# Reordering one GpSimd addition and one ScalarE copy, and reducing softmax's maximum and sum in one operation each

## The chip, the cores and the metric

One core of one Trainium2 chip runs the whole program. The metric is device time in microseconds, the median of several runs. The engines are TensorE (PE in the profile, its weight loads PEld), VectorE (DVE), ScalarE (ACT), GpSimd (POOL) and the DMA queues (SP issues most of them). Each engine runs its own instructions in the order in which they are written; they meet only at semaphores.

## What is computed

The input is `x` of 4 sequences of 2048 rows of 256 float32 values. The result is a sandwich of three residual layers:

```
x = x + 0.5 * ffn(layernorm(x))     # gate: top 2 of 8 experts, each 256x256
x = x + attn(layernorm(x))          # 16 heads of 16; a row attends to itself and its two neighbours
x = x + 0.5 * ffn(layernorm(x))     # the same weights as the first

idx    = stack([(i - 1) % s, i, (i + 1) % s], axis=1)
scores = einsum('bshd,bsnhd->bshn', q, k[:, idx])      # three scores for each row and head
attn   = softmax(scores, axis=-1)
out    = einsum('bshn,bsnhd->bshd', attn, v[:, idx])
```

The experts are all computed and then weighted by a gate that is zero for the six not chosen. Softmax is over three values, so the kernel holds `score` and `prob` as [128 rows, 3, 2 x 16]: the three neighbours stand 32 values apart.

## The kernel before

The 8192 rows are 64 tiles of 128, handled as 32 pairs. A software pipeline of 37 steps (`s` from -1 to 35) runs over the pairs; the program is unrolled. In one step the engines work on several pairs at once: the first FFN of pair s, the attention projections of pair s-1, scores of group s-2, the output projection and the third layer norm of group s-3, and the second FFN of group s-4. A step in the middle of the kernel is a fixed, hand-written order of calls for each engine.

TensorE, in a middle step (`body`, last block): first FFN t=0 (24 matmuls of 512 columns), transposes TA, first FFN t=1, the 16 gate matmuls (L930), transposes TO, q/k/v (24 matmuls), output projection (12 matmuls into tr_bank), gate transpose (L939), second FFN's first bank, bias matmuls (L955), 24 more matmuls, transposes TD, 18 more, transposes TB. All FFN products go through four PSUM banks, `ffn_bank`, so the next product into a bank waits until ScalarE (even banks, `scale_step`, L446) or VectorE (odd banks, `chain_step`, L656) has read it. Every product is made of a high and a low part: ScalarE copies the transposed operand rounded to `T_hi` (`hi_step`, L409), VectorE subtracts it to get `T_lo` (`lo_step`, L579), and TensorE waits for `T_lo`. The output projection waits for `T_lo` of TO (L579), which VectorE makes in the middle of the gate's chain of small operations (L593 to L636).

VectorE, in a middle step: the second half of softmax (`weights_step(s-3, 1)`, L707 to L713), first FFN's sums (`chain_step`, which for its first bank needs GpSimd's `base`), values (L724 to L736), the gate, norm statistics, scores (L678 to L688), second FFN's sums, and between them the first half of softmax (`weights_step(s-2, 0)`: maximum L699, L701; subtraction L703), then `T_lo` of TD.

GpSimd, in a middle step: sums of the first FFN, then `rstd` of the second and third norms with `base` of the second FFN between them, `x1_bo`, `rstd` of the first norm for pair s+2 (ends with L314), then the sums of the second FFN (`sum_step`, L332, L334, L340, twice), then `base_step(FFN1, s+1)` (L324), then two gathers of rows of x (L383).

ScalarE, in a middle step: ..., `scale_step(FFN2, s-4, 0)`, `normalise_step(LN3, s-3)`, `exp_step(s-2)` (L487, waits for the subtraction L703), `hi_step(TD, s-3)` (waits for TensorE's transposes TD), `scale_step(FFN2, s-4, 1)` (L446), `hi_step(TB, s)`.

At the end (steps 31 to 33) VectorE runs both halves of softmax and the value step within one step (`drains`), since there is no further pair to hide them behind. From step 32 on there is no first FFN.

`idle` (L558) is a two-element copy that keeps two dependent VectorE operations apart.

Of the kernel before, what the change touches and what calls it, by code (L numbers as in the profile page):

```python
# [22 lines left out]
B, S, D, H, E = 4, 2048, 256, 16, 8  # L23
DH = D // H
PART = 128
# [52 lines left out]
def build(nc, x, Wp, bp, Wq, bq, Wk, bk, Wv, bv, Wo, bo, We, be, Wg, bg, out):  # L78
# [9 lines left out]
    with ExitStack() as ctx:  # L88
        def sb(name, shape, dt=f32):
            return ctx.enter_context(nc.sbuf_tensor(name, shape, dt))  # L90
# [63 lines left out]
        moved_x1_bo = sb("moved_x1_bo", [PART, 2, D])  # L154
        prod = sb("prod", [PART, 3, 2, D])
        score, prob = sb("score", [PART, 3, 2 * H]), sb("prob", [PART, 3, 2 * H])
        most = sb("most", [PART, 2, 2 * H])
        total = sb("total", [PART, 3, 2 * H])
        attn = sb("attn", [PART, 2, D])
        x2 = sb("x2", [PART, 2, 2, D])  # L160
        y = sb("y", [PART, 2, 2, D])
# [115 lines left out]
        def _(pool):  # L277
# [38 lines left out]
            def base_step(f, n):  # L316

                if f == FFN1:
                    await_x(pool, n)
                else:  # L320
                    pool.wait_ge(x2_done, n.times(1, 1))
                pool.wait_ge(bias_copied[f], n.times(1, 1))
                await_(pool, chain_done[f], n.times(8))
                nc.gpsimd.tensor_tensor(base[:, f], (x_in if f == FFN1 else x2)[:, n.slot], bias_sum[:, f],  # L324
                                        ALU.add).then_inc(base_done[f], 1)
# [32 lines left out]
            def body(s):  # L358
# [9 lines left out]
                    x1_bo_step(s - 1)  # L368
                if (s + 2).within(PAIRS):
                    rstd_step(LN1, s + 2)  # L370
                if (s - 4).within(GROUPS):
                    sum_step(FFN2, s - 4, 0)
                    sum_step(FFN2, s - 4, 1)
                if (s + 1).within(PAIRS):
                    base_step(FFN1, s + 1)
                n = s + 3
                if n.within(PAIRS):
                    if n.const == 2:
# [12 lines left out]
        def _(act):  # L391
# [114 lines left out]
            def body(s):  # L506
# [31 lines left out]
                    scale_step(FFN2, s - 4, 0)  # L538
                if (s - 3).within(GROUPS):
                    normalise_step(LN3, s - 3)  # L540
                if (s - 2).within(GROUPS):
                    exp_step(s - 2)
                if (s - 3).within(GROUPS):
                    hi_step(TD, s - 3)
                if ffn2:
                    scale_step(FFN2, s - 4, 1)
                if ffn1 and not filling:
# [6 lines left out]
        def _(dve):  # L554
# [136 lines left out]
            def weights_step(a, part):  # L691
                ops = attn_ops

                def after(k):
                    dve.wait_ge(ops, a.times(ATTN_OPS, k))

                if part == 0:
                    after(4)
                    nc.vector.tensor_tensor(most[:, 0], score[:, 0], score[:, 1], ALU.max).then_inc(ops, 1)  # L699
                    after(5)  # L700
                    nc.vector.tensor_tensor(most[:, 1], most[:, 0], score[:, 2], ALU.max).then_inc(ops, 1)  # L701
                    after(6)
                    nc.vector.tensor_tensor(score[:], score[:], most[:, 1].unsqueeze(1).to_broadcast([PART, 3, 2 * H]),  # L703
                                            ALU.subtract).then_inc(ops, 1)
                else:
                    dve.wait_ge(exp_done, a.times(1, 1))
                    nc.vector.tensor_tensor(total[:, 0], prob[:, 0], prob[:, 1], ALU.add).then_inc(ops, 1)  # L707
                    after(8)
                    nc.vector.tensor_tensor(total[:, 1], total[:, 0], prob[:, 2], ALU.add).then_inc(ops, 1)
                    after(9)  # L710
                    nc.vector.reciprocal(total[:, 2], total[:, 1]).then_inc(ops, 1)
                    after(10)
                    nc.vector.tensor_tensor(prob[:], prob[:], total[:, 2].unsqueeze(1).to_broadcast([PART, 3, 2 * H]),  # L713
                                            ALU.mult).then_inc(ops, 1)

            def value_step(a):
# [365 lines left out]
```

## Time and profile before

| | us |
|---|---|
| median of 3 runs | 1137.74 (1134.66 to 1139.28) |
| the profiled execution, its own time | 1135.11 |
| its span from first to last instruction | 1133.3, mean granted TensorE clock 0.976 |
| busy: TensorE matmul | 1070.8 (94%) |
| busy: TensorE weight load | 889.8 (79%) |
| busy: VectorE | 950.8 (84%) |
| busy: GpSimd | 714.8 (63%) |
| busy: ScalarE | 518.8 (46%) |

A matmul of 512 columns is listed as 0.39 us long, but the next one starts 0.23 us later: the listed times overlap, and a busy TensorE is not a TensorE without gaps. Gaps are read from the starts of its instructions, one after the other. A row of the timeline gives start, duration, engine, line, operation, what is written and read, the count, and in brackets the idle time before it and what ended that. A row of the chain gives start, duration and what. In the page's second part the granted clock of TensorE is full through the middle and falls at the start and in the last tenth of the span.

### The profile page before, as it was taken

The numbers are of one execution on the slowest core, as the hardware profiler recorded it, in microseconds if no ns is written. First come the engines' busy times: TensorE is split into PE (matmuls) and PEld (weight loads), VectorE is DVE, ScalarE is ACT, GpSimd is POOL, SyncE is SP. The second block draws the span as 40 slices with busy tenths as digits, with TensorE's granted clock in tenths as the row PEclk, the third lists the DMA queues.
The fourth block names the chain that finished last, engine by engine and source line by source line (L and its number), as shares of the span: only waits on it lengthen the run. The fifth ranks groups of instructions, "written<-read, shape, count | busy, mean of one in ns | idle before, by whom it ended". The sixth has DMA issues, their size and how long they took to land.

```text
span 1133.3 us, 17965 instructions
## 1 busy us (share of the span) xinstructions
PE 1070.8 (94%) x5459; PEld 889.8 (79%) x5459; DVE 950.8 (84%) x2675; ACT 518.8 (46%) x1181; POOL 714.8 (63%) x953
## 2 busy tenths in 40 slices
PE   4898799999999999999999999999999999998785
PEld 2676688888888888888888888888888888887563
DVE  3659789898898898888888989888889898988873
ACT  3253454444455544544555444445554444444331
POOL 2465466666676666666766676667666766563443
PEclk9899899999999999999999999999999999999988
DMA  5001000000000000000000000000000000000000
GB/s 162 10 30 35 12 15 6 19 20 20 19 19 20 14 6 19 20 19 20 20 19 11 10 19 20 19 20 19 20 12 8 19 20 20 10 10 10 10 10 19
DMA packets 12583, 23.05 MB, mean 20 GB/s; under 512 B 2212, under 2 KB 5812, under 8 KB 12488
## 3 DMA queue, kind: packets, MB, share of 16 engines
q1 hardware_dynamic: 9240, 13.37, 3.4%
q0 software_dynamic: 3248, 8.54, 2.7%
q8 instruction: 44, 0.72, 0.3%
q14 instruction: 51, 0.42, 0.1%
HBM read 12.47 MB, written 8.39 MB: 18 GB/s over the span
## 4 chain that ended last, share of the span: by engine, by line
PE 80%; DVE 9%; SPq 3%; DMA 2%; issue 2%; ACT 2%; POOL 1%; DVEq 0%; POOLq 0%; ACTq 0%
PE ffn_bank L889 18%; PE ffn_bank L891 18%; PE ffn_bank L890 18%; PE tr_bank L918 5%; PE tr_bank L930 4%; PE mix_bank L890 3%; PE mix_bank L891 3%; PE mix_bank L889 3%; SPq L243 2%; PE tr_bank L889 2%; DVE chain_sum L656 2%; PE mix_bank L955 1%; DMA we_raw<-in_L_ffn_We 1%; PE tr_bank L891 1%; PE tr_bank L890 1%
## 5 line engine op out<-in xcount | busy, mean ns | idle before, releaser
L889 PE MATMUL ffn_bank<-we_hi,T_hi 128*128 128x512 f32 x1024 | 416.3, 407 | 3.8 <-DVE chain_sum L656 2.5
L891 PE MATMUL ffn_bank<-we_hi,T_lo 128*128 128x512 f32 x1024 | 404.9, 395 | 0.0
L890 PE MATMUL ffn_bank<-we_lo,T_hi 128*128 128x512 f32 x1024 | 404.0, 395 | 0.0
L332 POOL TENSOR_TENSOR chain_sum<-chain_sum,we_raw 128x512 f32<-128x512 f32 x128 | 165.8, 1295 | 184.4 <-DVE chain_sum L656 184.4
L446 ACT ACTIVATE we_raw<-ffn_bank,gate 128x256 f32<-128x256 f32 x512 | 208.1, 479 | 134.7 <-PE ffn_bank L891 134.6
L889 PEld LDWEIGHTS ffn_bank<-we_hi,T_hi 128*128 128x128 f32 x1024 | 195.3, 191 | 46.1 <-issue 4.6
L891 PEld LDWEIGHTS ffn_bank<-we_hi,T_lo 128*128 128x128 f32 x1024 | 194.5, 190 | 43.2
L890 PEld LDWEIGHTS ffn_bank<-we_lo,T_hi 128*128 128x128 f32 x1024 | 195.6, 191 | 35.5
L409 ACT CAST T_hi<-tr_bank 128x512 fp32r<-128x512 f32 x128 | 75.0, 588 | 121.8 <-PE tr_bank L918 121.6
L656 DVE SCALAR_TENSOR_TENSOR chain_sum<-ffn_bank,gate,base 128x256 f32<-128x256 f32 x128 | 61.4, 479 | 77.2 <-POOL base L324 49.3
L656 DVE SCALAR_TENSOR_TENSOR chain_sum<-ffn_bank,gate,chain_sum 128x256 f32<-128x256 f32 x256 | 110.7, 473 | 8.4 <-PE ffn_bank L891 8.4
L334 POOL TENSOR_TENSOR pool_sum<-chain_sum,we_raw 128x256 f32<-128x256 f32 x128 | 108.4, 847 | 10.0
L309 POOL TENSOR_TENSOR var_eps<-mean_var,eps 128x2 f32<-128x2 f32 x96 | 20.7, 216 | 144.1 <-DVE mean_var L574 144.1
L579 DVE TENSOR_TENSOR T_lo<-tr_bank,T_hi 128x512 fp32r<-128x512 f32 x128 | 87.0, 682 | 27.6 <-ACT T_hi L409 27.6
L889 PE MATMUL mix_bank<-wqkv_hi,T_hi 128*128 128x512 f32 (+1 forms) x256 | 90.1, 352 | 5.0 <-ACT qk L470 5.0
L558 DVE COPY idle<-minus_half 128x2 f32<-128x2 f32 x170 | 85.6, 504 | 5.9
L891 PE MATMUL mix_bank<-wqkv_hi,T_lo 128*128 128x512 f32 (+1 forms) x256 | 87.9, 343 | 0.0
L890 PE MATMUL mix_bank<-wqkv_lo,T_hi 128*128 128x512 f32 (+1 forms) x256 | 87.8, 343 | 0.0
L383 POOL DMA_INDIRECT x_in<-in_L_attn_x,x_row x60 | 66.9, 1115 | 18.2 <-issue 9.1
L312 POOL TENSOR_TENSOR rstd<-var_eps,minus_half 128x2 f32<-128x2 f32 x96 | 77.0, 802 | 0.0
L429 ACT ACTIVATE normed<-x,shift,rstd 128x256 f32<-128x256 f32 x128 | 70.6, 609 | 6.4 <-POOL shift L314 6.3
L918 PE MATMUL tr_bank<-ident,normed 128*128 128x128 f32 x384 | 59.9, 281 | 8.0 <-ACT normed L429 7.9
(128 smaller groups left out, 1862.2 us busy)
## 6 DMA issues: line engine op xcount, KB each, us to landing
out_x<-y SPq DMA_DIRECT2D x31, 256.0 KB, 2.0
we_raw<-in_L_ffn_We SPq DMA_DIRECT2D x2, 1024.0 KB, 13.9
x_in<-in_L_attn_x,x_row POOLq DMA_INDIRECT x60, 2.9
x_in<-in_L_attn_x SPq DMA_DIRECT2D x2, 256.0 KB, 7.5
moved_qk<-qk SPq DMA_DIRECT2D x4, 124.0 KB
w_raw<-in_L_attn_Wq SPq DMA_DIRECT2D x1, 256.0 KB, 2.8
w_raw<-in_L_attn_Wk SPq DMA_DIRECT2D x1, 256.0 KB, 3.0
w_raw<-in_L_attn_Wv SPq DMA_DIRECT2D x1, 256.0 KB, 3.9
```

The costliest lines, as they stand in the source:

```text
L312: nc.gpsimd.tensor_tensor(rstd[:, ln], var_eps[:, ln], minus_half[:], ALU.pow).then_inc(done, 1)
L332: nc.gpsimd.tensor_tensor(chain_sum[:, f, t], chain_sum[:, f, t], scaled[:, f, t, 1], ALU.add).then_inc(done, 1)
L334: nc.gpsimd.tensor_tensor(pool_sum[:, f, t], chain_sum[:, f, t, 0], scaled[:, f, t, 0, 1], ALU.add).then_inc(done, 1)
L409: nc.scalar.copy(halves(i, n)[0][:].rearrange("p t k n -> p (t k n)"), t_bank[i][:, :]).then_inc(hi_done[i], 1)
L446: last = nc.scalar.activation(scaled[:, f, t, half, j], ffn_bank[b][:, j * D:(j + 1) * D], ACT.Copy, scale=gate[:, 2 * f + t, e:e + 1])
L558: nc.vector.tensor_copy(idle[:], minus_half[:])
L579: nc.vector.tensor_tensor(lo[:].rearrange("p t k n -> p (t k n)"), t_bank[i][:, :], hi[:].rearrange("p t k n -> p (t k n)").bitcast(f32), ...
L656: nc.vector.scalar_tensor_tensor(out=chain_sum[:, f, t, j], in0=ffn_bank[b][:, j * D:(j + 1) * D], scalar=gate[:, 2 * f + t, e:e + 1], in1 ...
L889: nc.tensor.matmul(dest, hi[:, t, k, :], w_hi_[:, k, c0:c1], start=(first and k == 0), stop=False, skip_group_check=not first)
L890: nc.tensor.matmul(dest, hi[:, t, k, :], w_lo_[:, k, c0:c1], start=False, stop=False, skip_group_check=not first)
L891: last = nc.tensor.matmul(dest, lo[:, t, k, :], w_hi_[:, k, c0:c1], start=False, stop=(k == KB - 1), skip_group_check=not first)
L918: last = nc.tensor.transpose(t_bank[i][:, at:at + PART], source[:, t, k * PART:(k + 1) * PART], ident[:])
```

## The change

Four edits. GpSimd's `base_step(FFN1, s + 1)` moves in front of the two `sum_step(FFN2, ...)`. ScalarE's `hi_step(TD, s - 3)` moves in front of `exp_step(s - 2)`. The maximum over the three scores becomes one `tensor_reduce` along a view in which the three are innermost (stride 32 values), in place of two `tensor_tensor`; so does the sum over the three exponentials. The semaphore's counts stay as they were (the reduction adds 2).

```diff
@@ gpsimd, body
                     rstd_step(LN1, s + 2)
+                if (s + 1).within(PAIRS):
+                    base_step(FFN1, s + 1)
                 if (s - 4).within(GROUPS):
                     sum_step(FFN2, s - 4, 0)
                     sum_step(FFN2, s - 4, 1)
-                if (s + 1).within(PAIRS):
-                    base_step(FFN1, s + 1)
@@ scalar, body
                     normalise_step(LN3, s - 3)
+                if (s - 3).within(GROUPS):
+                    hi_step(TD, s - 3)
                 if (s - 2).within(GROUPS):
                     exp_step(s - 2)
-                if (s - 3).within(GROUPS):
-                    hi_step(TD, s - 3)
@@ vector, weights_step
                     after(4)
-                    nc.vector.tensor_tensor(most[:, 0], score[:, 0], score[:, 1], ALU.max).then_inc(ops, 1)
-                    after(5)
-                    nc.vector.tensor_tensor(most[:, 1], most[:, 0], score[:, 2], ALU.max).then_inc(ops, 1)
+                    nc.vector.tensor_reduce(most[:], score[:].rearrange("p m h -> p h m"), AX.X, ALU.max).then_inc(ops, 2)
                     after(6)
...
                     dve.wait_ge(exp_done, a.times(1, 1))
-                    nc.vector.tensor_tensor(total[:, 0], prob[:, 0], prob[:, 1], ALU.add).then_inc(ops, 1)
-                    after(8)
-                    nc.vector.tensor_tensor(total[:, 1], total[:, 0], prob[:, 2], ALU.add).then_inc(ops, 1)
+                    nc.vector.tensor_reduce(total[:, 0], prob[:].rearrange("p m h -> p h m"), AX.X, ALU.add).then_inc(ops, 2)
                     after(9)
```

The subtraction, the reciprocal and the multiplication that follow read `most` and `total` at their new places and are otherwise the same.

## Rows read from the trace of the kernel before

**Rows 1.** Windows: busy us and (count) of PE, PEld, DVE, ACT, POOL; clock; DMA
```profile
483.00:516.00 33.00, 33.00 (x174) 27.71 (x172) 29.29 (x82) 15.76 (x36) 23.09 (x30) 1.00 0.05 17
```

**Rows 2.** Timeline of PE, step 13: gate matmuls, projection, second FFN's first bank
```profile
432.00 0.28 PE L930 MATMUL tr_bank<-wg,T_hi 128*128 128x16 f32 x2
...
438.48 0.39 PE L889 MATMUL tr_bank<-wo_hi,T_hi 128*128 128x256 f32 x1
...
440.18 0.47 PE L889 MATMUL ffn_bank<-we_hi,T_hi 128*128 128x512 f32 x1
```

**Rows 3.** Timeline of PE, step 4: the same three instructions
```profile
140.94 0.28 PE L930 MATMUL tr_bank<-wg,T_hi 128*128 128x16 f32 x2
...
147.34 0.28 PE L889 MATMUL tr_bank<-wo_hi,T_hi 128*128 128x256 f32 x1
...
148.81 0.48 PE L889 MATMUL ffn_bank<-we_hi,T_hi 128*128 128x512 f32 x1
```

**Rows 4.** Timeline of DVE: first gate operation in step 4, then step 13 with T_lo
```profile
142.82 0.19 DVE L593 TENSOR_TENSOR logits<-tr_bank,bg_all 128x32 f32<-128x32 f32 x1 [0.81 <-PE tr_bank L930]
...
434.64 0.17 DVE L593 TENSOR_TENSOR logits<-tr_bank,bg_all 128x32 f32<-128x32 f32 x1
...
437.75 0.68 DVE L579 TENSOR_TENSOR T_lo<-tr_bank,T_hi 128x512 fp32r<-128x512 f32 x1
```

**Rows 5.** Waits, whole span: who waited for whom, us in total, times, longest
```profile
DVE chain_sum L656 <- POOL base L324: 49.3, 28, 2.0
```

**Rows 6.** Timeline of POOL, step 13: last rstd operation, base addition
```profile
448.46 0.19 POOL L314 TENSOR_TENSOR shift<-minus_mean,rstd 128x2 f32<-128x2 f32 x1
...
458.18 1.29 POOL L324 TENSOR_TENSOR base<-x_in,bias_sum 128x512 f32<-128x512 f32 x1
```

**Rows 7.** Timeline of PE: transposes TD, TB, TB and the matmul behind them
```profile
447.67 0.66 PE L918 MATMUL tr_bank<-ident,normed 128*128 128x128 f32 x4
448.08 0.49 PE L889 MATMUL ffn_bank<-we_hi,T_hi 128*128 128x512 f32 x1
...
452.31 0.60 PE L918 MATMUL tr_bank<-ident,normed 128*128 128x128 f32 x4
453.46 0.47 PE L889 MATMUL ffn_bank<-we_hi,T_hi 128*128 128x512 f32 x1 [0.55 <-ACT we_raw L446]
...
485.30 0.60 PE L918 MATMUL tr_bank<-ident,normed 128*128 128x128 f32 x4
485.79 0.47 PE L889 MATMUL ffn_bank<-we_hi,T_hi 128*128 128x512 f32 x1
```

**Rows 8.** Timelines of POOL, DVE and ACT, step 13: sum, maximum, subtraction, exponential, T_hi, scaling
```profile
449.57 1.29 POOL L332 TENSOR_TENSOR chain_sum<-chain_sum,we_raw 128x512 f32<-128x512 f32 x1 [0.92 <-DVE chain_sum L656]
...
449.62 1.29 DVE L701 TENSOR_TENSOR most<-most,score 128x32 f32<-128x32 f32 x1
450.94 0.84 DVE L703 TENSOR_TENSOR score<-score,most 128x96 f32<-128x96 f32 x1
...
451.82 0.29 ACT L487 ACTIVATE prob<-score 128x96 f32<-128x96 f32 x1 [4.21 <-DVE score L703]
452.01 0.57 ACT L409 CAST T_hi<-tr_bank 128x512 fp32r<-128x512 f32 x1
452.47 0.48 ACT L446 ACTIVATE we_raw<-ffn_bank,gate 128x256 f32<-128x256 f32 x1
```

**Rows 9.** The chain that ended last, steps 31 and 32
```profile
1031.17 1.30 DVE most L701
...
1033.44 0.85 ACT we_raw L446 x2
...
1042.06 0.43 PE mix_bank L890
```

**Rows 10.** Source lines L688 and L707: count, ns min/median/max, first and last start, form
```profile
L688 DVE TENSOR_REDUCE score<-prod x32: 1733/1740/1753, 95.6 to 1079.2; 128x96 f32<-128x1536 f32 x32
...
L707 DVE TENSOR_TENSOR total<-prob x32: 178/908/921, 98.8 to 1086.5; 128x32 f32<-128x32 f32 x32
```

More of the change, by code:

```diff
@@ L156, in build @@
         score, prob = sb("score", [PART, 3, 2 * H]), sb("prob", [PART, 3, 2 * H])
-        most = sb("most", [PART, 2, 2 * H])
-        total = sb("total", [PART, 3, 2 * H])
+        most = sb("most", [PART, 2 * H])
+        total = sb("total", [PART, 2, 2 * H])
         attn = sb("attn", [PART, 2, D])
@@ L698, in weights_step @@
                     after(4)
-                    nc.vector.tensor_tensor(most[:, 0], score[:, 0], score[:, 1], ALU.max).then_inc(ops, 1)
-                    after(5)
-                    nc.vector.tensor_tensor(most[:, 1], most[:, 0], score[:, 2], ALU.max).then_inc(ops, 1)
+                    nc.vector.tensor_reduce(most[:], score[:].rearrange("p m h -> p h m"), AX.X, ALU.max).then_inc(ops, 2)
                     after(6)
-                    nc.vector.tensor_tensor(score[:], score[:], most[:, 1].unsqueeze(1).to_broadcast([PART, 3, 2 * H]),
+                    nc.vector.tensor_tensor(score[:], score[:], most[:].unsqueeze(1).to_broadcast([PART, 3, 2 * H]),
                                             ALU.subtract).then_inc(ops, 1)
@@ L706, in weights_step @@
                     dve.wait_ge(exp_done, a.times(1, 1))
-                    nc.vector.tensor_tensor(total[:, 0], prob[:, 0], prob[:, 1], ALU.add).then_inc(ops, 1)
-                    after(8)
-                    nc.vector.tensor_tensor(total[:, 1], total[:, 0], prob[:, 2], ALU.add).then_inc(ops, 1)
+                    nc.vector.tensor_reduce(total[:, 0], prob[:].rearrange("p m h -> p h m"), AX.X, ALU.add).then_inc(ops, 2)
                     after(9)
-                    nc.vector.reciprocal(total[:, 2], total[:, 1]).then_inc(ops, 1)
+                    nc.vector.reciprocal(total[:, 1], total[:, 0]).then_inc(ops, 1)
                     after(10)
-                    nc.vector.tensor_tensor(prob[:], prob[:], total[:, 2].unsqueeze(1).to_broadcast([PART, 3, 2 * H]),
+                    nc.vector.tensor_tensor(prob[:], prob[:], total[:, 1].unsqueeze(1).to_broadcast([PART, 3, 2 * H]),
                                             ALU.mult).then_inc(ops, 1)
```

## The prediction

> **What bounds the kernel now.** I read the windows first, in stretches of 33 us, one step of the pipeline each. In the middle of the kernel TensorE is busy for 33.00 of 33.00 us at full clock, VectorE for 29.3, GpSimd for 23.1, ScalarE for 15.8 [rows 1]; the 26 windows from 153 to 1011 us are all like this one, with never less than 32.45 us of TensorE. Taken at its word this says that no other engine matters there, and that the change can only help at the two ends. But matmuls overlap in the record, so a gap of some tenths between two of them does not show as idle time. So I read TensorE's timeline by the starts of its instructions, and compared the same piece of work in different steps.
>
> Two places in the middle are longer than the work in them. The first lies around the output projection. From the first gate matmul to the second FFN's first matmul takes 440.18 - 432.00 = 8.18 us in step 13 [rows 2] and 148.81 - 140.94 = 7.87 us in step 4 [rows 3], for the same 16 gate matmuls, transposes, q/k/v, projection and gate transpose at the same clock. The difference, 0.31 us, has a cause in the row of VectorE: the projection starts at 438.48 [rows 2], and `T_lo`, its operand, was finished at 437.75 + 0.68 = 438.43 [rows 4]. TensorE waits for VectorE there. VectorE is late because it comes late to the gate: its first gate operation starts 434.64 - 432.00 = 2.64 us behind the first gate matmul in step 13, against 142.82 - 140.94 = 1.88 us in step 4, where it sat waiting for TensorE [rows 2 to 4].
>
> The second place is the end of a step. Behind the transposes TD the next matmul starts after 448.08 - 447.67 = 0.41 us; behind the transposes TB after 0.49 us in step 14, and after 1.15 us in step 13, where the row itself names ScalarE's L446 as what it waited for [rows 7]. Of the 23 such transitions I read (steps 6 to 28), these are the shortest and the longest; their mean is 0.58 us, 0.17 us over the 0.41.
>
> What stands before that L446 is a chain [rows 8]: second maximum (L701, from 449.62), subtraction (L703), exponential, `T_hi` of TD, then L446 at 452.47. It takes 2.85 us. In the drain, the same chain takes 1033.44 - 1031.17 = 2.27 us, and there it is on the chain that ended last [rows 9].
>
> **The base addition.** VectorE waits for it in 28 steps, 49.3 us in total, up to 2.0 us [rows 5]. The addition runs at 458.18, though the last `rstd` operation in front of its new place ends at 448.46 + 0.19 = 448.65 [rows 6] and its inputs (x gathered in an earlier step, the bias copied before the second norm's scaling) are there. At its new place it runs at about 448.7 to 450.0. What is queued behind it: the first of the FFN2 sums, which now starts at 449.57 [rows 8], moves by 0.4 us; the outputs' stores hang on it, and nothing on TensorE. The gathers stand behind the sums as before and no longer have the addition right ahead of them, so they are not later. VectorE's wait goes. What is late next for it: TensorE's own banks. Its first gate operation then comes as soon as the logits do, 1.88 instead of 2.64 us behind [rows 3, 4], and `T_lo` is up to 0.76 us earlier, where the projection lacks only some 0.3. So the projection's stall goes: 0.31 us in steps 5 to 31, 27 x 0.31 = 8.4 us.
>
> **The maximum.** L701 takes 1.29 us for 32 elements, and ends with GpSimd's L332 (449.57 + 1.29 = 450.86; L701 ends at 450.91). The subtraction then takes 0.84 us in the face of the next GpSimd sum [rows 8]. So it is not arithmetic that is paid here but the wait of an operation with two inputs for GpSimd. The new reduction has one input. The nearest row is L688, 1.74 us for 1536 elements to 96 sums, with hardly any scatter (1733 to 1753 ns) although it meets GpSimd's work too [rows 10]. That bounds the reduction of 96 elements to 32 results: 1.74 x 96 / 1536 = 0.11 us if elements count, 1.74 x 32 / 96 = 0.58 us if results count. I take 0.25, nearer to the lower end since a result here has 3 elements and not 16. Either way it ends while GpSimd's sum runs, and the subtraction (two inputs) inherits the 1.29 us wait. What is saved is the second operation of the pair: from the start of L701 to L446 there remain 1.29 + 0.04 to the exponential and, with `T_hi` out of the way, 0.19 to L446, together 1.52 us. That is 2.85 - 1.52 = 1.33 us less where the subtraction met GpSimd a second time, 2.27 - 1.52 = 0.75 us less where it didn't [rows 8, 9].
>
> The Trainium skill says the same of the wait ("Advanced Engine Details and Errata", GPSIMD Details): GpSimd shares a read and a write interface with VectorE, in conflict with VectorE instructions that have two SBUF inputs. By that rule the wait passes on to the subtraction; without it the drain's gain below would be some 3.7 us larger.
>
> **ScalarE's copy ahead of the exponential.** It waits for the transposes TD, which start at 447.67 and are over before 448.4 [rows 7], when the exponential can't start before about 450. ScalarE is idle for 4.21 us there [rows 8]. So the copy costs nothing at its new place; the 0.46 us between its start and L446 (452.47 - 452.01) are in the 1.33 and 0.75 above. If the transposes were later than the score, the exponential would wait behind the copy; by these rows they have 1.5 us in hand.
>
> Together these two edits bring L446 0.75 to 1.33 us forward, over the 0.74 us (1.15 - 0.41) that TensorE waited at the worst. So the stall behind TB goes: 27 steps (4 to 30) x 0.17 = 4.6 us.
>
> **The sum of the exponentials.** In the middle VectorE meets GpSimd there (median 0.91 us), in the drain it doesn't (0.18) [rows 10]. Two additions of 0.18 give way to one reduction of 0.11 to 0.58: between 0.25 us gained and 0.22 lost for each of three drain steps; at 0.25 for the reduction it is 0.1 each, 0.3 in all. In the middle the slack above hides it.
>
> The Trainium skill speaks against these views ("Vector Engine (DVE) Microarchitecture Reference", 5.2 Measured stream behaviour on trn2): a stream in single words with steps between them falls to 2.5 ns per column. An estimate by that page is 0.32 us for a reduction, and 0.1 us instead of 0.3 us gained in the drain. No row here shows such a stream.
>
> **The ends.** In the filling steps the base addition does not move past anything (there is no second FFN yet) and what ends last is the transfer of the moved q and k, which does not depend on softmax; I count nothing. In steps 31 to 33 the softmax chain is on the path: 0.75 us in each of 31 and 32 [rows 9], and 1.33 in 33, which repeats the form of rows 8. That is 2.8 us, with the sum 3.1.
>
> **The sum.** 1135.1 (the profiled execution) - 8.4 - 4.6 - 3.1 = 1119.0 us. The median of the runs shown is 2.6 us above that execution; I forecast 1119, 1.6% below the median.
>
> **The rivals.**
> One stall stays (1124 to 1128): the base addition now runs into the moment when the subtraction wants its turn, and if GpSimd's next sum gets in first, as at 450.94 [rows 8], the subtraction waits a second time, and the stall behind TB stays: 1135.1 - 8.4 - 3.1 = 1123.6. Or VectorE, early now, has its value products fall on GpSimd's sums and gives the time back before the gate: 1135.1 - 4.6 - 3.1 = 1127.4. Against it: L701 waited and got its turn as soon as L332 ended.
>
> Drain alone (1132): the middle is bound by TensorE as the windows say [rows 1], and my 0.31 and 0.17 us are its own way of starting, not waits: 1135.1 - 3.1 = 1132.0. Against it speaks that `T_lo` ends 0.05 us before the projection starts [rows 2, 4].
>
> Slower (about 1155): the reduction over three strided elements is dear. The chain from the first maximum to L446 takes about 2.5 us in the shorter form (2.27 from the second maximum [rows 9], and some 0.2 for the first); with a reduction of R it takes R + 0.5. From R = 2.0 us the stall behind TB grows by what lies above, in 27 steps; with the projection's gain set against it, the kernel is slower from R = 2.3. At R = 3 it is 27 - 8.4 = 19 us slower. The bound of 0.58 from L688 speaks against it.
>
> Clock: behind idle gaps of some us in the drain a matmul comes every 0.43 us instead of 0.23, nine in a row at 1042 [rows 9], 1.8 us for each such stretch. Shorter gaps may spare one or two, moved ones may add one: 1115 to 1121.
>
> **Chances.** Forecast 0.50, forecast with stretches at half clock spared 0.06 (1115), one stall stays 0.24, drain alone 0.14, slower 0.06. The range has to leave out no more than 0.2: 1113 to 1132, where the upper end takes in the drain alone in part. A measurement of this kernel can tell about 0.5% from no change; against the median that is 1132.05, so the drain alone falls half and half: faster 0.50 + 0.06 + 0.24 + 0.07 = 0.87, same 0.07, slower 0.06.
>
> **What would show it.** In the profile after, VectorE's wait for L324 is gone from the waits; the projection starts 0.12 us after the last v matmul and `T_lo` is over some tenths before; behind TB the next matmul starts after 0.41 us; a middle step lasts some 0.5 us less. L703 takes about 1.3 us and ends with a GpSimd operation; the reductions take 0.2 to 0.4 us. It is wrong if the middle steps keep their length, or if a reduction takes over a microsecond.

## The result and the profile after

The changed kernel takes 1116.49 us (median of 6 runs, 1115.0 to 1119.13) beside 1136.62 us for the kernel before (6 runs, 1133.9 to 1139.49). The ratio is 0.982, with a 95% interval of 0.980 to 0.985: 1.8% faster. The forecast was 1119.0 us. The profiled execution took 1119.13 us with a span of 1117.1 us, beside 1135.11 and 1133.3 before. It is the slowest of the six, and the one before is faster than the median: the medians are 20.1 us apart, the two profiles 16.0. What follows divides up the 16.0; about the other 4 us no trace says anything.

First the page of the changed kernel, busy us of each engine and its share of the span:

```profile
PE 1055.4 (94%) x5459; PEld 884.0 (79%) x5459; DVE 904.2 (81%) x2611; ACT 528.1 (47%) x1181; POOL 714.0 (64%) x953
```

Then the window that [rows 1] shows of before (columns as there):

```profile
483.00:516.00 33.00, 33.00 (x175) 27.95 (x175) 28.20 (x83) 17.29 (x39) 23.37 (x31) 1.00 0.05 17
```

TensorE is busy for 33.00 of 33.00 us in both kernels, and yet a step of the pipeline has become shorter. The windows can't show this, since they don't see tenths between overlapping matmuls. The starts do. TensorE's timeline after, step 13 of the pipeline (start, us, line, operands), against [rows 2, 7]:

```profile
429.43 0.28 PE L926 MATMUL tr_bank<-wg,T_hi 128*128 128x16 f32 x2
...
435.82 0.28 PE L885 MATMUL tr_bank<-wo_hi,T_hi 128*128 128x256 f32 x1
...
437.29 0.48 PE L885 MATMUL ffn_bank<-we_hi,T_hi 128*128 128x512 f32 x1
...
449.42 0.60 PE L914 MATMUL tr_bank<-ident,normed 128*128 128x128 f32 x4
449.77 0.48 PE L885 MATMUL ffn_bank<-we_hi,T_hi 128*128 128x512 f32 x1
```

From the first gate matmul to the second FFN's first matmul it now takes 437.29 - 429.43 = 7.86 us; before it took 8.18 there and 7.87 in step 4 [rows 2, 3]. Behind the transposes TB the next matmul starts after 449.77 - 449.42 = 0.35 us, not 0.49 to 1.15 [rows 7]. The other engines in the same step:

```profile
429.63 0.88 DVE L656 SCALAR_TENSOR_TENSOR chain_sum<-ffn_bank,gate,chain_sum 128x256 f32<-128x256 f32 x2 [1.19 <-PE ffn_bank L887]
431.31 0.19 DVE L593 TENSOR_TENSOR logits<-tr_bank,bg_all 128x32 f32<-128x32 f32 x1 [0.81 <-PE tr_bank L926]
433.51 0.68 DVE L579 TENSOR_TENSOR T_lo<-tr_bank,T_hi 128x512 fp32r<-128x512 f32 x1
...
445.72 1.30 POOL L324 TENSOR_TENSOR base<-x_in,bias_sum 128x512 f32<-128x512 f32 x1
446.98 1.31 POOL L332 TENSOR_TENSOR chain_sum<-chain_sum,we_raw 128x512 f32<-128x512 f32 x1
...
446.53 0.24 DVE L699 TENSOR_REDUCE most<-score 128x32 f32<-128x96 f32 x1
446.81 0.32 DVE L701 TENSOR_TENSOR score<-score,most 128x96 f32<-128x96 f32 x1
...
445.48 0.59 ACT L409 CAST T_hi<-tr_bank 128x512 fp32r<-128x512 f32 x1 [0.75 <-PE tr_bank L914]
447.17 0.28 ACT L487 ACTIVATE prob<-score 128x96 f32<-128x96 f32 x1 [1.10 <-DVE score L701]
447.36 0.46 ACT L446 ACTIVATE we_raw<-ffn_bank,gate 128x256 f32<-128x256 f32 x1
```

VectorE's first gate operation starts 431.31 - 429.43 = 1.88 us behind the first gate matmul, and it sat waiting for TensorE, as in step 4 before [rows 4]. `T_lo` ends at 434.19, 1.63 us ahead of the projection; before it was 0.05 [rows 2, 4]. The base addition stands at 445.72, directly ahead of the first FFN2 sum. `T_hi` is out of the way 1.1 us before the exponential, and L446 follows the exponential after 0.19 us instead of 0.65 [rows 8].

Over all middle steps (6 to 29), before and after: a step lasts 32.39 and 31.84 us. From gate to FFN2 it is 8.21 and 7.87, behind TB 0.58 and 0.35. The two places give 0.34 + 0.23 = 0.57, the step 0.55. The whole execution, by the gate transpose's copy (L421) of each step: up to step 4 149.1 and 151.1 us (+2.0), steps 4 to 30 842.0 and 827.7 (-14.2), step 30 to 31 31.4 and 30.5 (-0.9), from there to the end of the last arithmetic instruction 102.5 and 99.5 (-3.0). Behind it the last store and the end of the program take 8.4 us in both. Step 13, from which most rows of before are taken, is an unusual one: it is the only one of the middle steps 6 to 29 in which the subtraction L703 takes 0.84 us; in the others it takes 0.26.

### The profile page after: what moved, and what is told of

It reads as the page before. It is cut to its first block, busy times and chain, and to the rows that moved or that the text cites. A ratio compares the mean times of both kernels' runs of the same rounds, so it can differ in the third digit from the quotient of the medians.

```text
span 1117.1 us, 17965 instructions
## 1 busy us (share of the span) xinstructions
PE 1055.4 (94%) x5459; PEld 884.0 (79%) x5459; DVE 904.2 (81%) x2611; ACT 528.1 (47%) x1181; POOL 714.0 (64%) x953
## 4 chain that ended last, share of the span: by engine, by line
PE 84%; DVE 6%; SPq 3%; DMA 2%; issue 2%; ACT 1%; POOL 0%; POOLq 0%; DVEq 0%; ACTq 0%
PE ffn_bank L885 19%; PE ffn_bank L887 19%; PE ffn_bank L886 19%; PE tr_bank L914 5%; PE tr_bank L926 4%; PE mix_bank L885 4%; PE mix_bank L886 4%; PE mix_bank L887 4%; SPq L243 2%; PE tr_bank L885 1%; PE tr_bank L886 1%; PE tr_bank L887 1%; PE mix_bank L951 1%; DMA we_raw<-in_L_ffn_We 1%; DMA moved_x_bo<-x_bo 1%
## 5 line engine op out<-in xcount | busy, mean ns | idle before, releaser
L446 ACT ACTIVATE we_raw<-ffn_bank,gate 128x256 f32<-128x256 f32 x512 | 209.1, 473 | 139.3 <-PE ffn_bank L887 138.3
L309 POOL TENSOR_TENSOR var_eps<-mean_var,eps 128x2 f32<-128x2 f32 x96 | 20.6, 215 | 146.4 <-DVE mean_var L574 146.4
L334 POOL TENSOR_TENSOR pool_sum<-chain_sum,we_raw 128x256 f32<-128x256 f32 x128 | 104.4, 816 | 10.0
L324 POOL TENSOR_TENSOR base<-x,bias_sum 128x512 f32<-128x512 f32 x32 | 42.1, 1316 | 70.3 <-issue 55.7
L383 POOL DMA_INDIRECT x_in<-in_L_attn_x,x_row x60 | 71.6, 1193 | 15.2 <-issue 13.2
L558 DVE COPY idle<-minus_half 128x2 f32<-128x2 f32 x170 | 75.9, 447 | 5.9
```

Source lines behind the costliest of these rows:

```text
L334: nc.gpsimd.tensor_tensor(pool_sum[:, f, t], chain_sum[:, f, t, 0], scaled[:, f, t, 0, 1], ALU.add).then_inc(done, 1)
L383: nc.gpsimd.indirect_dma_start(out=x_in[:, n.slot, t, :], out_offset=None, in_=x_rows[:, :], in_offset=bass.IndirectOffsetOnAxis(ap=x_row[ ...
L446: last = nc.scalar.activation(scaled[:, f, t, half, j], ffn_bank[b][:, j * D:(j + 1) * D], ACT.Copy, scale=gate[:, 2 * f + t, e:e + 1])
L558: nc.vector.tensor_copy(idle[:], minus_half[:])
```

## The experiments

The forecast rests on two stalls of TensorE that are counted one by one: one that the late base addition causes (the projection, 8.4 us), one that softmax and ScalarE's copy cause (behind TB, 4.6 us). The kernels below make the parts alone or leave one out. All of them have the same arithmetic unless told otherwise. Medians in us; "before" is the kernel before, run alongside; steps are means over 6 to 29, "gate-FFN2" and "behind TB" the two places above. The drain (the copy of step 31 to the end of the last arithmetic) and the steps are of one profile each; the drain moves with the stretches in which the granted clock is half. Medians, not profiles, say which kernel is faster.

| kernel | median | before | ratio (95%) | step | gate-FFN2 | behind TB | drain |
|---|---|---|---|---|---|---|---|
| before | 1136.62 | | | 32.39 | 8.21 | 0.58 | 102.5 |
| base_only | 1139.4 | 1139.68 | 1.0008 (0.9989-1.0027) | 32.41 | 7.87 | 0.95 | 102.9 |
| hi_alone | 1121.41 | 1135.4 | 0.9867 (0.9851-0.9884) | 31.92 | 7.94 | 0.36 | 100.0 |
| max_alone | 1127.61 | 1135.4 | 0.9921 (0.9903-0.9939) | 32.17 | 8.17 | 0.38 | 101.6 |
| sum_alone | 1132.52 | 1135.4 | 0.9973 (0.9963-0.9982) | 32.48 | 8.17 | 0.72 | 100.6 |
| max_and_sum (one run) | 1124.56 | 1135.4 | | 32.11 | 8.11 | 0.38 | 99.5 |
| all_but_softmax | 1128.04 | 1139.68 | 0.9917 (0.9893-0.9941) | 32.16 | 7.87 | 0.70 | 99.8 |
| all_but_hi | 1117.95 | 1139.68 | 0.9824 (0.9799-0.9848) | 31.87 | 7.87 | 0.38 | 98.4 |
| all_but_base | 1117.54 | 1139.68 | 0.9826 (0.9801-0.9851) | 31.84 | 7.88 | 0.35 | 97.4 |
| after | 1116.49 | 1136.62 | 0.9824 (0.9802-0.9846) | 31.84 | 7.87 | 0.35 | 99.5 |

### The base addition alone (base_only)

```diff
 rstd_step(LN1, s + 2)
+base_step(FFN1, s + 1)
 sum_step(FFN2, s - 4, 0)
 sum_step(FFN2, s - 4, 1)
-base_step(FFN1, s + 1)
```

> The kernel before with the base addition moved and nothing else. Theory (two separate stalls of TensorE in a middle step: the projection's, set by VectorE that waited for the base addition, and the one behind the transposes TB, set by the softmax chain on ScalarE): the first goes, the second stays. A middle step of 32.39 us becomes 32.05 to 32.1, the drain keeps its length, about 1128 us where before has 1136.6. Rival (the base addition's 2 us were all of VectorE's lateness, everything follows from it): a middle step of 31.84 as in the changed kernel, about 1121 us.

Measured: 1139.4 beside 1139.68 us, ratio 1.0008. The projection's stall is gone in all steps (7.87 us), as the forecast had it, and the kernel is no faster. Neither the theory (32.05 to 32.1 us a step) nor the rival (31.84) came out: it is 32.41. The timelines of POOL, DVE, ACT and PE of this kernel, step 13 (its gate transpose's copy starts at 442.19):

```profile
450.34 1.29 POOL L324 TENSOR_TENSOR base<-x_in,bias_sum 128x512 f32<-128x512 f32 x1
451.59 1.29 POOL L332 TENSOR_TENSOR chain_sum<-chain_sum,we_raw 128x512 f32<-128x512 f32 x1
...
451.15 0.53 DVE L699 TENSOR_TENSOR most<-score 128x32 f32<-128x32 f32 x1
451.71 1.22 DVE L701 TENSOR_TENSOR most<-most,score 128x32 f32<-128x32 f32 x1
452.96 0.26 DVE L703 TENSOR_TENSOR score<-score,most 128x96 f32<-128x96 f32 x1
...
453.25 0.29 ACT L487 ACTIVATE prob<-score 128x96 f32<-128x96 f32 x1 [3.90 <-DVE score L703]
...
454.00 0.60 PE L918 MATMUL tr_bank<-ident,normed 128*128 128x128 f32 x4
454.90 0.47 PE L889 MATMUL ffn_bank<-we_hi,T_hi 128*128 128x512 f32 x1 [0.30 <-ACT we_raw L446]
```

The first maximum ends with the base addition (451.68 and 451.63), the second with the sum behind it (452.93 and 452.88). The pair needs 1.78 us and starts into one GpSimd operation more than before. The second half of L446 comes 11.7 to 11.9 us behind the copy of the gate transpose instead of 11.4 (medians of odd and even steps), and TensorE waits for it behind TB: 0.95 us on average instead of 0.58. What the projection gives, 0.34 us, TB takes, 0.37.

### All but the base addition (all_but_base)

The edit is the changed kernel with `base_step(FFN1, s + 1)` back behind the two FFN2 sums.

> The changed kernel with the base addition at its old place. Theory: the stall behind TB goes, the projection's stays, and the drain gains its 3 us: a middle step of about 32.15 us, about 1127 us. Rival (it is VectorE's work that counts, and the reductions take some 1.7 us per step of it away): VectorE reaches the gate early in spite of the wait, 31.84 us per step, about 1118 us.

Measured: 1117.54 beside 1139.68 us, ratio 0.9826, a middle step of 31.84 us, the same as with all four parts. The rival came out. The wait of VectorE for the base addition is not only still there, it is longer than in [rows 5]:

```profile
DVE chain_sum L656 <- POOL base L324: 78.5, 28, 2.9
```

(waits over the whole span: us in total, times, longest). It costs nothing now. VectorE comes 2.13 us behind the first gate matmul instead of 2.68, and `T_lo` is ready 0.49 us ahead of the projection on average instead of 0.06. The same kernel's timelines of DVE, ACT and POOL in step 13:

```profile
444.92 0.25 DVE L699 TENSOR_REDUCE most<-score 128x32 f32<-128x96 f32 x1
445.20 1.28 DVE L701 TENSOR_TENSOR score<-score,most 128x96 f32<-128x96 f32 x1
...
446.52 0.28 ACT L487 ACTIVATE prob<-score 128x96 f32<-128x96 f32 x1 [2.06 <-DVE score L701]
446.71 1.55 ACT L446 ACTIVATE we_raw<-ffn_bank,gate 128x256 f32<-128x256 f32 x4
...
445.08 1.29 POOL L332 TENSOR_TENSOR chain_sum<-chain_sum,we_raw 128x512 f32<-128x512 f32 x1 [0.92 <-DVE chain_sum L656]
...
452.35 1.30 POOL L324 TENSOR_TENSOR base<-x_in,bias_sum 128x512 f32<-128x512 f32 x1
```

Here the subtraction pays the 1.28 us as forecast (it ends at 446.48, GpSimd's sum at 446.37), and the base addition is still 7.3 us behind it. But it comes 16.4 us behind the gate transpose's copy and not 17.1: whatever brings L446 forward brings VectorE's sums, GpSimd's sums and with them the base addition forward.

### The copy alone (hi_alone)

```diff
 normalise_step(LN3, s - 3)
-exp_step(s - 2)
 hi_step(TD, s - 3)
+exp_step(s - 2)
```

> The kernel before with ScalarE's third-norm operand ahead of the exponential and nothing else. Theory now (one root: L446 of the second FFN's second half, held up by the softmax chain, delays both TensorE behind TB and, by way of VectorE's sums, GpSimd's sums and the base addition behind them, VectorE's start into the next step and so the projection): L446 comes 0.46 us earlier, the stall behind TB goes in the short form of the chain, the base addition comes up to 0.46 us earlier and most of the projection's stall goes too; a middle step of 31.9 to 32.0 us against 32.39 before and 31.84 after, the drain 1 to 1.4 us shorter, about 1122 us. Rival (two separate causes, the projection's stall needs the base addition moved): 32.15 to 32.2 us, about 1129 us.

Measured: 1121.41 beside 1135.4 us, ratio 0.9867, as this theory had it. A middle step takes 31.92 us: 0.47 of the 0.55 us come from exchanging two instructions of ScalarE. ScalarE's timeline, step 13, and TensorE's behind TB:

```profile
446.44 0.58 ACT L409 CAST T_hi<-tr_bank 128x512 fp32r<-128x512 f32 x1 [0.75 <-PE tr_bank L918]
449.30 0.28 ACT L487 ACTIVATE prob<-score 128x96 f32<-128x96 f32 x1 [2.28 <-DVE score L703]
449.49 1.55 ACT L446 ACTIVATE we_raw<-ffn_bank,gate 128x256 f32<-128x256 f32 x4
...
450.37 0.60 PE L918 MATMUL tr_bank<-ident,normed 128*128 128x128 f32 x4
450.72 0.48 PE L889 MATMUL ffn_bank<-we_hi,T_hi 128*128 128x512 f32 x1
```

L446 follows 0.19 us behind the exponential, with the copy long done. The first time of the second half moves from 11.4 to 10.9 us behind the gate transpose's copy. The same half microsecond can be followed round: the base addition goes from 17.1 to 16.6 us behind that copy and VectorE's first FFN1 sum of the next step from 18.5 to 18.0. TensorE, no longer held behind TB, is itself 0.2 us earlier at its next gate matmul (23.7 instead of 23.9 us behind the copy), so that of VectorE's 0.5 us there remain 0.3: its first gate operation goes from 2.68 to 2.39 us behind the gate matmul, and `T_lo` from 0.06 to 0.25 us ahead of the projection. So the place from gate to FFN2 shrinks to 7.94 us, by 0.27 of the 0.34, without the base addition being touched.

### The maximum, the sum, and both (max_alone, sum_alone, max_and_sum)

```diff
-nc.vector.tensor_tensor(most[:, 0], score[:, 0], score[:, 1], ALU.max).then_inc(ops, 1)
-after(5)
-nc.vector.tensor_tensor(most[:, 1], most[:, 0], score[:, 2], ALU.max).then_inc(ops, 1)
+nc.vector.tensor_reduce(most[:, 1], score[:].rearrange("p m h -> p h m"), AX.X, ALU.max).then_inc(ops, 2)
```

> The kernel before with the maximum as one reduction and nothing else. Theory of one root: the reduction takes 0.25 us, the subtraction takes over the wait for GpSimd (1.28 us), L446 comes 0.3 us earlier in the short form and 0.9 us in the long one, both stalls go nearly whole: 31.85 to 31.95 us per step, drain 1 to 1.5 us shorter, about 1121 us. Rival (two causes): 32.15 to 32.2 us, about 1129 us.

```diff
-nc.vector.tensor_tensor(total[:, 0], prob[:, 0], prob[:, 1], ALU.add).then_inc(ops, 1)
-after(8)
-nc.vector.tensor_tensor(total[:, 1], total[:, 0], prob[:, 2], ALU.add).then_inc(ops, 1)
+nc.vector.tensor_reduce(total[:, 1], prob[:].rearrange("p m h -> p h m"), AX.X, ALU.add).then_inc(ops, 2)
```

> The kernel before with the sum of the exponentials as one reduction and nothing else. Theory of one root: the 0.85 us per step that VectorE saves lie before its wait for the base addition, which grows by as much; the middle step stays at 32.39 us, the drain loses 0.1 us per step at most: within 1 us of before. Rival (VectorE's work counts): 32.1 to 32.2 us per step, about 1130 us.

The third kernel has both.

> The kernel before with both reductions and nothing else. Theory of one root: as with the maximum alone, 31.85 to 31.95 us per step, the sum adds nothing in the middle. Rival (the sum's 0.85 us count once the maximum is out of the way): at least 0.1 us per step less than with the maximum alone.

Measured: the maximum alone gives 0.22 us a step (32.17), nearly all of it behind TB (0.38 us). The subtraction takes 1.28 us in place of the second maximum and ends 0.22 us earlier, which is the first maximum saved; the base addition moves by 0.23 us and the place from gate to FFN2 by 0.04. This is what the rival with two causes had forecast (32.15 to 32.2 us), not the theory of one root. The reason stands in the starts: VectorE's first FFN1 sum is 0.23 us earlier, TensorE's next gate matmul 0.18, so only 0.05 us reach the gate (2.63 instead of 2.68). An earlier L446 shortens the projection's stall only by what it gives over TensorE's own gain behind TB.

The sum alone: in its profile a middle step is no shorter (32.48 us, +0.09), since the subtraction loses its turn to GpSimd more often (0.84 us in place of 0.26 in 6 of the 24 steps; in the kernel before in one), and behind TB it is 0.72 us. But that profile is of the slowest of its ten executions (1135.89 us), and the median is 2.9 us under before, with a ratio whose interval lies below 1. So the sum alone gains some 0.3%; no trace shows where. Both together: 32.11 us, 0.28 us a step.

### Leaving out the copy, and leaving out both reductions (all_but_hi, all_but_softmax)

Each is the changed kernel with one part as it was before: `exp_step` ahead of `hi_step(TD, ...)`, or the pairs of maxima and additions.

> The changed kernel with ScalarE's third-norm operand behind the exponential again. Theory: L446 comes some 0.46 us later than in the changed kernel, which the middle has in hand, so 31.84 to 31.9 us per step; the drain loses 3 x 0.46 = 1.4 us: about 1118 us against 1116.5. Rival (the copy's place is what removed the stall behind TB): 32.05 us per step, about 1124 us.

> The changed kernel with the two-operation maximum and sum. Theory: 31.84 to 31.95 us per step, since the copy's new place alone is worth 0.46 us against a mean stall of 0.2; the drain keeps 3 x 0.46 of its 3 us: about 1118.5 us. Rival (the second maximum's wait for GpSimd, now with the base addition in front of the sums, keeps ScalarE late): 32.05 us per step, about 1124 us.

Measured: 1117.95 and 1128.04 us beside 1139.68, ratios 0.9824 and 0.9917; 31.87 and 32.16 us a step. The first is as its theory had it; the second is slower than theory and rival. Without the copy's move the kernel loses 0.03 us a step, though that move alone gave 0.47. Without the reductions, base addition and copy together give 0.23 us, less than the copy alone (0.47): with the pair of maxima the early base addition costs 0.24 us a step. With the reductions it is the other way round: they give 32.11 us without it (max_and_sum) and 31.87 with it (all_but_hi). There the exponential starts 9.6 to 9.7 us behind the gate transpose's copy instead of 10.5, because the subtraction gets in between the base addition and the sum and doesn't wait a whole GpSimd operation. That brings L446 early enough without the copy's move, so copy and early addition stand in for each other. So the parts don't add. Alone they give -0.02, 0.47, 0.22 and -0.09 us, a sum of 0.58 that is close to the 0.55 of all four only by chance: copy, maximum and sum without the base addition already give 0.55. By the ratios of whole executions the four alone give 1.3, 0.8, 0.3 and -0.1%, together 2.3, and all four at once 1.8%.

### What the base addition is good for (slack_all, slack_no_base)

Both get a needless reduction of `prod` (1.74 us on VectorE, its result is not used) in each middle step, behind the values' sum and ahead of the first FFN's sums of the second tile.

```diff
+filler = sb("filler", [PART, 96])
...
+if s.const < PAIRS - 1:
+    nc.vector.tensor_reduce(filler[:], prod[:].rearrange("p m t (h d) -> p (m t h) d", d=DH), AX.X, ALU.add)
```

On the changed kernel:

> The changed kernel with one more reduction of 1.74 us on VectorE in every middle step, behind the values' sum (its result is not used). Theory: in the changed kernel VectorE waits 1.1 us for TensorE at its next sum but one and has the projection's operand ready 1.6 us ahead; together more than 1.74, so a middle step stays at 31.84 us. Rival (VectorE is close to its limit): the step grows by 0.2 us or more.

On all_but_base:

> The same extra reduction of 1.74 us in the kernel that has everything but the moved base addition. Theory: the step was 31.84 us there too, but the operand was ready only 0.44 us ahead and VectorE did not wait for TensorE; so the step grows by 1.74 - 0.44 = 1.3 us, to about 33.1 us, and the moved addition is worth its margin alone. Rival (the moved addition is of no use at all): as in the run beside it.

Measured, one run each: 1118.65 and 1155.03 us, a middle step of 31.84 and 33.28 us. The changed kernel takes up 1.74 us a step and shows nothing of it; without the base addition's move 1.43 us of it stand on TensorE (forecast: 1.3). The filler, VectorE's `T_lo` and TensorE's gate and projection, first in slack_all:

```profile
427.12 1.74 DVE L815 TENSOR_REDUCE filler<-prod 128x96 f32<-128x1536 f32 x1
...
433.43 0.68 DVE L580 TENSOR_TENSOR T_lo<-tr_bank,T_hi 128x512 fp32r<-128x512 f32 x1
...
428.98 0.28 PE L929 MATMUL tr_bank<-wg,T_hi 128*128 128x16 f32 x2
...
435.37 0.28 PE L888 MATMUL tr_bank<-wo_hi,T_hi 128*128 128x256 f32 x1
```

then in slack_no_base:

```profile
440.59 1.74 DVE L815 TENSOR_REDUCE filler<-prod 128x96 f32<-128x1536 f32 x1
...
446.91 0.68 DVE L580 TENSOR_TENSOR T_lo<-tr_bank,T_hi 128x512 fp32r<-128x512 f32 x1
...
440.14 0.28 PE L929 MATMUL tr_bank<-wg,T_hi 128*128 128x16 f32 x2
...
447.64 0.39 PE L888 MATMUL tr_bank<-wo_hi,T_hi 128*128 128x256 f32 x1 [0.94 <-DVE T_lo L580]
```

With the addition early, the filler is over before the gate matmuls begin (428.86 and 428.98), and `T_lo` is ready 435.37 - 434.11 = 1.26 us ahead of the projection. With the addition late, the filler only starts at 440.59, behind the first gate matmul, and the row of the projection names `T_lo` (ready at 447.59). So the base addition's move gives a margin of over a microsecond on VectorE's side, but in this kernel, once L446 is early, no time.

### The arrangement of the elements (sum_contiguous)

The sum's reduction takes three adjacent elements instead of three with 32 elements between them. It adds the wrong values; count and size are the same.

```diff
-nc.vector.tensor_reduce(total[:, 0], prob[:].rearrange("p m h -> p h m"), AX.X, ALU.add).then_inc(ops, 2)
+nc.vector.tensor_reduce(total[:, 0], prob[:].rearrange("p m h -> p (m h)").rearrange("p (h m) -> p h m", m=3), AX.X, ALU.add).then_inc(ops, 2)
```

> The changed kernel with the sum of the exponentials taken over three adjacent values instead of three that stand 32 apart (this adds up the wrong ones; all else is computed). Theory: steps of single words cost a reduction of 96 elements nothing that shows, 0.25 us in both. Rival (the Trainium skill, Vector Engine (DVE) Microarchitecture Reference, 5.2: single words with steps between them are read at less than the full rate): the adjacent one takes 0.05 to 0.15 us less.

Measured: 1117.59 us in one run, 31.83 us a step. Source line L705 (count, ns min/median/max, first and last start), in the changed kernel and then in this one:

```profile
L705 DVE TENSOR_REDUCE total<-prob x32: 251/255/261, 99.1 to 1069.8; 128x32 f32<-128x96 f32 x32
```

```profile
L705 DVE TENSOR_REDUCE total<-prob x32: 241/243/253, 98.5 to 1068.4; 128x32 f32<-128x96 f32 x32
```

The strided form costs 12 ns more for 96 elements.

### The idling copy of one element (idle_one)

The chain that ended last goes through an instruction of VectorE whose result nothing reads: the copy L558, which the code puts behind some of VectorE's waits to keep them apart. It has two elements; this kernel, on top of the changed one, copies one.

```diff
-nc.vector.tensor_copy(idle[:], minus_half[:])
+nc.vector.tensor_copy(idle[:, 0:1], minus_half[:, 0:1])
```

> The changed kernel with the spacing copies (L558) of one element instead of two. Theory: the two-element copy waits for GpSimd's running instruction because it uses the interface that the two engines share, a one-element copy doesn't; the copies take 0.17 us always, the wait passes in part to the next operation with two SBUF inputs (L605), and the gate's chain becomes 1.0 to 1.5 us shorter in each of the drain steps 32 to 34, where it is on the path; the middle stays at 31.84 us: 3 to 4 us less than the changed kernel, about 1113 us. Rival (the wait is that of any operation that writes SBUF, or it passes on whole): the copies still take up to 1.1 us, or L605 takes over 1 us, and the time stays at 1116.5.

Measured: 1114.03 us (1112.56 to 1114.83) beside 1136.59, ratio 0.9803, 95% interval 0.9790 to 0.9817. The changed kernel's own is 0.9824 (0.9802 to 0.9846): this is likely the faster of the two by 0.2%, but the intervals overlap, and the two did not run side by side. Source line L558 in the changed kernel, then here:

```profile
L558 DVE COPY idle<-minus_half x170: 168/170/1281, 11.3 to 1093.0; 128x2 f32<-128x2 f32 x170
```

```profile
L558 DVE COPY idle<-minus_half x170: 153/154/157, 12.0 to 1086.6; 128x1 f32<-128x1 f32 x170
```

The copy of two elements takes up to 1.28 us, the copy of one never over 0.157; VectorE's time in this line falls from 75.9 to 26.1 us. The wait passes on in part, as the theory had it: the next operation with two SBUF inputs, L605, has a median of 0.66 us instead of 0.34, and never more than 0.67; in the drain, where the copies waited longest, it takes mostly 0.37 us. The chain that ended last shows where that counts, in the changed kernel's drain (start, us, engine, line):

```profile
1053.06 1.07 DVE idle L558
1054.31 0.62 DVE idle L558
```

The pair comes again in each of the next two steps of the drain, at 1075.21 and 1091.78. That is 1.69 us in each of three steps, 4 us over what two copies of 0.154 take. None of them is on the chain of idle_one. Its drain is 6.4 us shorter, 93.1 us; there it also has no half-clock stretch, of which the changed kernel has two. The 6.4 us are of the fastest of its five executions beside the slowest of six: the medians differ by 2.5 us. In the middle it loses 0.11 us a step, 2.8 us in 26: every other step TensorE now waits 0.2 us ahead of the transposes TD. Part of the cause stands in the timelines of POOL and DVE:

```profile
406.17 1.30 POOL L324 TENSOR_TENSOR base<-x,bias_sum 128x512 f32<-128x512 f32 x1 [1.75 <-issue]
407.42 0.65 POOL L309 TENSOR_TENSOR var_eps<-mean_var,eps 128x2 f32<-128x2 f32 x1
...
406.50 2.12 DVE L678 TENSOR_TENSOR prod<-qk 128x512 f32<-128x512 f32 x2
```

A VectorE that is earlier starts its two-input products into GpSimd's base addition of the second FFN and holds the small steps behind it: L309 takes 0.65 us, at a usual 0.20, and the chain of the third norm behind it is late. Between 200 and 950 us L309 takes over 0.5 us 12 times of 70, every second step, and never in the changed kernel. That the 0.2 us ahead of TD are this and nothing else was argued from these rows and not tried. Nor was the one-element copy tried with the base addition at its old place.

## Why the prediction was right, and where it was wrong

**Middle and drain in size: right.** Forecast were 8.4 + 4.6 = 13.0 us for the steps 4 to 31 and 3.1 for the drain; measured 14.2 + 0.9 = 15.1 and 3.0, and 2.0 lost in the filling steps. The sum is off by 2.5 us at the median. That it is off by only 0.1 at the profiled execution is luck: this is the slowest of the six, and 2.0 us of it lie in the filling steps.

**The attribution: wrong.** The step that failed is in the base addition's paragraph: the sum behind it "moves by 0.4 us; the outputs' stores hang on it, and nothing on TensorE". TensorE does hang on it, by way of the contention that the very next paragraph describes: the maxima wait for GpSimd's running operation, the exponential waits for them, L446 for the exponential, and TensorE for L446. The prediction used this for the maximum and did not apply it to the addition that it had just moved there. With that, "27 x 0.31 = 8.4 us" for the base addition fell to nothing (base_only, 1.0008, half-width of 0.2%). The rival that one stall stays names nearly this ("the base addition now runs into the moment when the subtraction wants its turn"). In base_only it is the two maxima that run into it, the subtraction takes 0.26 us, and the stall behind TB does not only stay but grows.

**Two stalls that hang together.** The forecast gave each stall a cause of its own. hi_alone cures the second whole and the first by four fifths without touching the base addition: the second L446 holds TensorE behind TB directly, and holds the projection by the long way of VectorE's sums, GpSimd's sums, the base addition, VectorE's start into the next step, the gate and `T_lo`. "`T_lo` finished 0.05 us before the projection starts" was read rightly, as was VectorE's late arrival; the wait for L324 [rows 5] was the last link of a chain and was taken for its beginning. One root for both is still too strong: max_alone brings L446 0.2 us forward, which cures the stall behind TB nearly whole and the projection's by only 0.04 us. all_but_base shows the same from the other side: that wait grows from 49.3 to 78.5 us and costs nothing.

**The maximum: right, with two sizes off.** The reduction takes 0.24 to 0.26 us, at a forecast of 0.25. "The subtraction inherits the 1.29 us wait" holds in all_but_base and max_alone (1.28) and in the drain of the changed kernel, on its chain that ended last:

```profile
1017.94 1.30 DVE score L701
...
1022.21 1.44 DVE prod L720 x4
```

In its middle steps it does not: there the subtraction takes 0.32 or 0.51 us (medians of even and odd steps), since the base addition ends just then and lets it in between two GpSimd operations. "L703 takes about 1.3 us" among the signs was thus wrong for 26 of the 32 groups. And the 1.33 us of the working, read from step 13, belong to one middle step in 24; in all_but_base, where the subtraction does wait the 1.28 us, L446 comes 0.7 us earlier than before, near the working's 0.75. The other size is the floor behind TB: 0.35 us, where the prediction took TD's 0.41. Hence 0.23 us a step and not 0.17.

**The copy: right, and undervalued.** It costs nothing at its place (1.1 us of room ahead of the exponential), and its 0.46 us were in the working, as part of a joint edit. Alone it carries 85% of the middle's gain and, by the ratios, three quarters of the whole. The forecast never asked what each part would give alone.

**The sum of the exponentials: no view on its own.** "In the middle the slack above hides it" holds with the other parts. Each drain step gains 0.15 us by it, at a forecast of 0.1. On the estimate of 0.32 us from the Trainium skill ("Vector Engine (DVE) Microarchitecture Reference", 5.2 Measured stream behaviour on trn2): the page's 2.5 ns per column were measured with both sources, or the destination, stepping by 24 words, so it did not fit a reduction with one source; the trace has 0.255 us strided beside 0.243 us adjacent, 0.12 ns for each element.

**The ends.** For the filling steps the forecast had "I count nothing". The profiles differ by 2.0 us there: TensorE waits 6.9 us for the moved q and k (L470) instead of 5.0. That this is the change is not shown. Up to step 4 the profiles of all kernels here lie between 148.3 and 151.4 us, and sum_contiguous, which differs from the changed kernel in one view alone, has 149.7 us and waits 5.4. With what the middle gave over the forecast (2.1 us) the 2.0 make the sum come out right, by luck.

In the drain softmax's part can be read. On VectorE it takes from the first maximum to the first value product 5.41, 5.42 and 6.00 us in steps 31 to 33 before, and 4.56, 4.55 and 4.55 after, 3.2 us less in all: 2.7 by the maximum and the copy (forecast 2.8) and 0.5 by the sum (0.3). For step 31 it can be followed on the two chains: after, by the rows at 1017.94 and 1022.21 above (subtraction and first product); before, by 1031.17 in [rows 9] and this row of the same chain:

```profile
1036.37 1.43 DVE prod L724 x4
```

The first maximum starts 0.21 us ahead of 1031.17, the reduction 0.29 us ahead of 1017.94. The drain as a whole is 3.0 us shorter, though the changed kernel also has two half-clock stretches fewer (before at 1042, 1073, 1086 and 1097 us, after at 1027 and 1079). What they gave back, and what took it away again, was not traced.

**The other rivals.** Drain alone would leave a middle step at 32.39 us; it is 31.84. Slower needed a reduction of 2.3 us; it takes 0.25.

## What to carry to other kernels

When a profile shows two stalls in a pipelined loop, follow each backwards across the step's border before adding their prices; here both hung on one late operation of ScalarE, and the exchange of two of its instructions paid 85% of what four edits paid in the middle, and three quarters of the whole. A move on a queue that is off the critical path is only free if nothing contends with it at its new place: ask which two-input operations of VectorE run then. The same move can cost or pay by what stands around it (0.24 us a step lost with the pair of maxima, 0.24 gained with the reduction). And where several edits cure one stall, measure them alone and left out one at a time; an edit that adds nothing may still be the one that makes room for the next (1.74 us of extra work a step unseen, beside 1.43 us of it paid).

## What the runs showed of the hardware

- Of VectorE's instructions that meet a GpSimd operation, those with two inputs in SBUF wait to its end, however small they are: 32 elements take 1.28 us instead of 0.18. So VectorE and GpSimd do not meet only at semaphores. The next one in the queue inherits the wait unless it falls between two GpSimd operations; at that border tenths decide between 0.26 and 0.84 us for the same subtraction.
- A copy of two elements, with one input, waits as well (up to 1.28 us); a copy of one element (0.154 us, at most 0.157 in 170) and the 96-element reductions (0.24 to 0.26 us in 32) do not. The Trainium skill's "Advanced Engine Details and Errata" (VectorE Performance Modes, Mode Summary) says that VectorE's second port is shared with GpSimd, and that GpSimd's instructions and VectorE's two-port mode, for which it wants source and destination in SBUF and counts that are both even, or both odd, equal and above one, block each other. The copies of one and of two elements agree with that.
- It works both ways: GpSimd's two-element L309 takes 0.65 us instead of 0.20 while VectorE's 512-element product runs (idle_one).
- Adjacent or 32 elements apart makes 12 ns of difference for a reduction of 96 elements (0.243 and 0.255 us).
